# Batch 0's norm, expert choice, ranks and first four scatters moved earlier at the end of attentions 3 and 4

## What is computed

```python
q = layernorm(x) @ w_q ; k, v = ctx @ w_kv            # 16 heads of 64, ctx of 154 tokens
x = x + softmax(q k^T * scale) v @ w_out               # attention
xn = layernorm(x)
logits = xn.reshape(-1, 128) @ wg                      # 2048 tokens, 8 experts
top_vals, top_idx = top_k(logits, 2)
weights = softmax(top_vals)
x = x + sum over the 2 choices of weights * expert(top_idx)(xn)
```

## Time and profile before

| | us |
|---|---|
| median of 3 runs | 1202.76 (1201.64 to 1203.77) |
| the profiled execution, its own time | 1204.15 |
| span of its trace | 1202.4 |
| busy: PE, DVE, ACT, POOL | 1024.1, 729.6, 641.0, 573.5 |
| mean granted TensorE clock | 0.912 of full |

### The profile page before, as it was taken

How to read it: one execution, slowest core, us unless ns; L and a number is a source line. 1 busy time by engine, 2 the same in 40 slices (tenths; PEclk the granted TensorE clock), 3 DMA queues, 4 the chain that set the end, 5 groups by cost and what they waited for, 6 DMA issues and landing times.

```text
span 1202.4 us, 21878 instructions
## 1 busy us (share of the span) xinstructions
PE 1024.1 (85%) x6653; PEld 790.4 (66%) x6653; DVE 729.6 (61%) x2451; ACT 641.0 (53%) x2115; POOL 573.5 (48%) x923
## 2 busy tenths in 40 slices
PE   4986999858899988968999997697599999976993
PEld 3864888735556567855677765686467777655993
DVE  5575344576766684277767777523876767754443
ACT  2215333336777834428887875233487888831231
POOL 5232566542000023548565666657475555664452
PEclk9986999967999987989999999698799999975997
DMA  2003456696910113220000000275200000014666
GB/s 64 13 19 99 149 166 194 213 139 232 388 37 2 36 45 116 65 68 19 1 19 2 19 2 25 69 221 146 73 19 2 2 1 2 2 41 124 190 209 189
DMA packets 116003, 102.83 MB, mean 86 GB/s; under 512 B 18027, under 2 KB 97571, under 8 KB 115888
## 3 DMA queue, kind: packets, MB, share of 16 engines
q1 hardware_dynamic: 104992, 82.45, 23.5%
q0 software_dynamic: 8448, 17.20, 4.3%
q10 hardware_dynamic: 2448, 1.80, 0.7%
HBM read 65.04 MB, written 36.36 MB: 84 GB/s over the span
## 4 chain that ended last, share of the span: by engine, by line
PE 57%; DVE 16%; POOL 8%; issue 6%; DMA 6%; ACT 5%; SPq 1%; DVEq 0%; POOLq 0%; ACTq 0%
PE ps L2695 4%; PE ps L2877 4%; PE ps L2697 4%; PE ps L2696 4%; PE ps L2891 4%; PE ps L2775 3%; PE ps L2788 3%; PE ps L3065 3%; DMA xr<-xr_d,src_i 2%; POOL yq_d L902 2%; PE ps L2905 2%; POOL xq_d L883 2%; ACT ex L1278 2%; PE ps L3416 2%; PE ps L3221 2%
## 5 line engine op out<-in xcount | busy, mean ns | idle before, releaser
L1278 ACT ACTIVATE ex<-ps,nmx 128x154 f32<-128x154 f32 x512 | 193.9, 391 | 70.2 <-DVE nmx L2199 68.7
L1065 POOL TENSOR_TENSOR pp<-ex,rc 128x256 f32<-128x256 f32 x256 | 157.6, 615 | 145.5 <-DVE rc L2204 144.7
L2199 DVE TENSOR_REDUCE nmx<-ps 128x2 f32<-128x308 f32 x256 | 119.4, 469 | 61.7 <-PE ps L2697 61.3
L2877 PEld LDWEIGHTS ps<-ident,pp 128*128 128x128 f32 x640 | 73.8, 142 | 57.5 <-POOL pp L1066 49.3
L2695 PE MATMUL ps<-kp,q_s 128*128 128x308 f32 x256 | 96.4, 377 | 14.9 <-ACT ex L1278 7.7
L902 POOL DMA_INDIRECT yq_d<-yq,ids_q x78 | 74.7, 957 | 71.6 <-DVE yq L1961 52.9
L1278 ACT ACTIVATION_READ_ACCUMULATOR ex<-ps,nmx 128x1 f32 x512 | 105.1, 205 | 0.0
L2877 PE MATMUL ps<-ident,pp 128*128 128x128 f32 x640 | 100.0, 280 | 4.8 <-POOL pp L1066 4.8
L1402 ACT ACTIVATE pe<-ps,nmx 128x154 f32<-128x154 f32 x256 | 84.4, 395 | 29.4 <-DVE nmx L2080 28.4
L872 POOL TENSOR_TENSOR ln_r<-ln_v,mhalf 128x4 f32<-128x4 f32 x32 | 34.7, 1084 | 95.7 <-DVE ln_v L1696 77.6
L2696 PE MATMUL ps<-kp,q_s 128*128 128x308 f32 x256 | 79.8, 312 | 0.0
(11 more groups left out here) (448 smaller groups left out, 2756.0 us busy)
## 6 DMA issues: line engine op xcount, KB each, us to landing
w_r<-in_L_ffn_W SPq DMA_DIRECT2D x69, 256.0 KB, 3.4
xq_d<-blankq SPq DMA_DIRECT2D x4, 4160.0 KB, 23.9
w_q<-in_L_ffn_W SPq DMA_DIRECT2D x46, 256.0 KB
w_q<-in_L_ffn_w SPq DMA_DIRECT2D x46, 128.0 KB
xq<-xq_d SPq DMA_DIRECT2D x22, 130.0 KB, 2.5
w_s<-in_L_ffn_W SPq DMA_DIRECT2D x8, 256.0 KB
w_e<-in_L_ffn_W SPq DMA_DIRECT2D x8, 256.0 KB, 5.1
acc<-yq_d SPq DMA_DIRECT2D x8, 256.0 KB, 4.5
```

What stands on the lines that cost most here:

```text
L1065: pool.tensor_tensor(pp[st % 2][:, m % 4, 2 * j:2 * j + 2, :], w[:, :, 0:P], r.broadcast_to([P, 2, P]), ALU.mult)
L1278: ins = act.activation(ex[:, tt % NEX, j, :], ps[:, tt % 3, j * SK:(j + 1) * SK], ACT.Exp, bias=nmx8[:, tt % 8, j:j + 1], accum_out=sm8[:, ...
L2199: dve.tensor_reduce(nmx8[:, tt % 8, :], ps[:, tt % 3, 0:2 * SK].rearrange("p (h s) -> p h s", h=2), AX.X, ALU.max, negate=True).then_inc(n ...
L2877: last = pe.transpose(ps[:, bank, k * P:(k + 1) * P], pp[st % 2][:, k, c, :], ident[:, :])
```

## The change

In attentions 3 and 4:

- Batch 0's `tail_shift` takes the place of its `tail_scale`, and `scale(l, 0)` runs on ScalarE behind the last exponentials of step 13. The count that `shifted` waits for grows with it.
- `tail_statistics` of batches 0 and 1 stand ahead of the maxima of tile 4 in steps 13 and 14, where they stood ahead of those of tile 7. Their `rstd` on GpSimd move from behind tile 7 to behind tile 4 (step 13) and tile 5 (step 14).
- Batch 0's `tail_xT` moves from the end of step 14 to behind its tile 1, its `logits` from step 15 into step 14, `best` ahead of tile 7 of step 14, `indices` and `marks` behind tile 7 of step 14.
- `rank(0)`, `shares(0)`, `ranks(0)` and `second_rows(0)` move from the tail into step 15.
- The first four of batch 0's eight scatters are issued by GpSimd in step 15, one behind each of the tiles 4 to 7. Batch 2's `rstd` still stands behind the second scatter of those in `region`.
- The places in the ring of banks move accordingly.

```diff
--- before.py
+++ after.py
@@ -73,12 +73,12 @@
 
     ORDER = [(g, b) for g in range(2) for b in range(B)] + [(2, 0), (2, 1), (3, 0), (3, 1), (2, 2), (3, 2), (2, 3), (3, 3)]
     LAST = [max(st for st in range(NST) if ORDER[st][1] == b) for b in range(B)]
-    BEHIND = {(0, "A"): [("x", 1)], (0, "C"): [("x", 2)], (2, "A"): [("x", 3)], (13, "A"): [("f", 0)], (14, "A"): [("f", 1)], (14, "D"): [("t", 0)], (15, "A"): [("lg", 0)], (15, "D"): [("t", 1)]}
+    BEHIND = {(0, "A"): [("x", 1)], (0, "C"): [("x", 2)], (2, "A"): [("x", 3)], (13, "A"): [("f", 0)], (14, "A"): [("f", 1), ("t", 0)], (14, "C"): [("lg", 0)], (15, "A"): [("rk", 0)], (15, "D"): [("t", 1)]}
 
     BEHIND1 = {(14, "D"): [("u", 0)], (15, "A"): [("f", 0)], (15, "D"): [("u", 1)]}
     TAIL = [("f", 1), ("t", 0), ("pt", NST - 1, 3), ("o", NST - 2), ("pt", NST - 1, 1), ("pt", NST - 1, 2), ("u", 2), ("pt", NST - 1, 4), ("f", 2), ("t", 1), ("t", 2), ("o", NST - 1), ("u", 3), ("f", 3), ("t", 3)]
     NEXT = [("next", 0, i) for i in range(PREPS)]
-    ENDING = [None, None] + [[("pt", NST - 1, 1), ("rk", 0), ("pt", NST - 1, 4), ("pt", NST - 1, 3), ("f", 2), ("lg", 1), ("y", NST - 2), ("pt", NST - 1, 2), ("rk", 1), ("t", 2), ("y", NST - 1), ("lg", 2), ("f", 3)]
+    ENDING = [None, None] + [[("pt", NST - 1, 1), ("pt", NST - 1, 4), ("pt", NST - 1, 3), ("f", 2), ("lg", 1), ("y", NST - 2), ("pt", NST - 1, 2), ("rk", 1), ("t", 2), ("y", NST - 1), ("lg", 2), ("f", 3)]
                              + NEXT[0:1] * (l == 2) + [("rk", 2), ("t", 3), ("lg", 3)] + NEXT[1:2] * (l == 2) + [("rk", 3)] + NEXT[2:] * (l == 2) for l in (2, 3)]
 
     def ring(l):
@@ -597,7 +597,7 @@
 
         def shifted(l, b):
 
-            return ln_shift, B + (B - 1) * (l - 2) + b
+            return ln_shift, B + B * (l - 2) + b + 1
 
         def nth(s):
 
@@ -884,9 +884,9 @@
 
             def region(l):
 
-                for i in range(2 * TB):
+                for i in range(4, 2 * TB):
                     scatter_rows(l, 0, i)
-                    if i == 1:
+                    if i == 5:
                         rstd(2 * l + 1, 2)
                 for i in range(2 * TB):
                     scatter_rows(l, 1, i)
@@ -1104,10 +1104,12 @@
                             low_x(3)
                         elif (st, m) == (4, 0):
                             row_ids()
-                        elif (st, m) == (13, 7):
+                        elif (st, m) == (13, 4):
                             rstd(2 * l + 1, 0)
-                        elif (st, m) == (14, 7):
+                        elif (st, m) == (14, 5):
                             rstd(2 * l + 1, 1)
+                        elif st == 15 and m >= 4:
+                            scatter_rows(l, 0, m - 4)
                     if st % B == 1 and st < NST - B:
                         if st >= 2:
                             pool.wait_ge(*full(l, ("y", st - 2)))
@@ -1323,9 +1325,15 @@
                         turned_x(1)
                     elif st == 2:
                         turned_x(3)
+                    elif st == 14:
+                        tail_xT(l, 0)
+                    elif st == 15:
+                        shares(l, 0)
                     exps(st, 2)
                     copy_pt(st - 1, 2)
                     exps(st, 3)
+                    if st == 15:
+                        second_rows(l, 0)
                     exps(st, 4)
                     exps(st, 5)
                     copy_pt(st - 1, 4)
@@ -1337,14 +1345,14 @@
                         scale(l, 1)
                     step_prep(st, 3)
                     exps(st, 7)
+                    if st == 13:
+                        scale(l, 0)
                     high_out(st - 1, 0)
-                    if st >= 14:
-                        tail_xT(l, st - 14)
+                    if st == 15:
+                        tail_xT(l, 1)
                     copy_pt(st, 0)
                 high_out(NST - 2, 1)
-                shares(l, 0)
                 copy_pt(NST - 1, 4)
-                second_rows(l, 0)
                 copy_pt(NST - 1, 2)
                 shares(l, 1)
                 high_out(NST - 1, 0)
@@ -2304,13 +2312,11 @@
                         tail_sum(l, st - 13)
                     elif st == 15:
                         tail_shift(l, 1)
-                        best(l, 0)
+                        ranks(l, 0)
                     maxima(st, 3)
                     copy_pt(st - 1, 3)
-                    if st == 14:
-                        tail_scale(l, 0)
-                    elif st == 15:
-                        indices(l, 0)
+                    if st in (13, 14):
+                        tail_statistics(l, st - 13)
                     maxima(st, 4)
                     if st == 0:
                         summed_up(3)
@@ -2326,17 +2332,19 @@
                     step_prep(st, 2)
                     if st == 0:
                         moments_half(3, 1)
-                    elif st in (13, 14):
-                        tail_statistics(l, st - 13)
-                    elif st == 15:
-                        marks(l, 0)
+                    elif st == 13:
+                        tail_shift(l, 0)
+                    elif st == 14:
+                        best(l, 0)
                     maxima(st, 7)
                     step_prep(st, 3)
+                    if st == 14:
+                        indices(l, 0)
+                        marks(l, 0)
                 maxima(NST, 0)
                 copy_pt(NST - 1, 1)
                 low_out(NST - 2, 0)
                 low_out(NST - 2, 1)
-                ranks(l, 0)
                 copy_pt(NST - 1, 3)
                 tail_sum(l, 2)
                 best(l, 1)
@@ -2942,8 +2950,10 @@
                         turned_x(3)
                     elif st in (13, 14):
                         tail_sum(l, st - 13, *summed(l, st - 13))
+                        if st == 14:
+                            tail_xT(l, 0)
                     elif st == 15:
-                        logits(l, 0)
+                        rank(l, 0)
                     scores(st, 2)
                     transposes(st - 1, 2)
                     scores(st, 3)
@@ -2956,17 +2966,18 @@
                     step_prep(st, 2)
                     if st == 0:
                         turned_x(2)
+                    elif st == 14:
+                        logits(l, 0)
                     scores(st, 6)
                     step_prep(st, 3)
                     scores(st, 7)
                     values(st - 1, 1)
                     rest_values(st - 1)
-                    if st >= 14:
-                        tail_xT(l, st - 14)
+                    if st == 15:
+                        tail_xT(l, 1)
                     transposes(st, 0)
                 st = NST - 1
                 transposes(st, 1)
-                rank(l, 0)
                 transposes(st, 4)
                 transposes(st, 3)
                 tail_sum(l, 2, *summed(l, 2))
```

## The result

| | us |
|---|---|
| before, median of 9 runs | 1204.07 (1201.64 to 1206.98) |
| changed, median of 9 runs | 1215.37 (1208.97 to 1221.07) |
| ratio | 1.0085, interval 1.0063 to 1.0107 |
| the profiled execution after, its own time | 1221.07 |
| span of its trace | 1219.3 |

The change makes the kernel slower, by 11.3 us on the medians, about twice the 5.1 us of the forecast, and outside its range.

The account below looks back on a forecast made before the run. The TensorE, ScalarE, VectorE chain to batch 3's variance and ranks bounds the tail. Steps plus GpSimd's scatters less the margin gave +2.36 and +2.78, together +5.14 us: 1207.9 us on the median of 1202.76, range 1202.5 to 1212.5.

Parts of the forecast that it names:

- Bound of the tail: Tail of both attentions: the TensorE, ScalarE, VectorE chain to batch 3's variance and ranks ends last; four fewer queued scatters buy nothing.
- 1.64 us as all that the boundary costs: Boundary 13/14, attention 3: ScalarE's batch 0 scalings delay the copy VectorE awaits, +1.64 us, bounds 0 and 1.64.
- the sentence on the statistics ahead of tile 4: Step 13: batch 0's statistics, 1.37 us, make the step wait about 1.06 us, covered at the boundary by the scalings' 1.64.
- Step 14: Attention 3: VectorE's scalings leave, -1.11; batch 1's statistics, `best` and `indices` 0; marks +1.26, idle time filled -1.17, TensorE's banks and logits +0.3.
- The 0.3 for the new order of the banks: TensorE in step 14: transposes 3 wait for `tail_sum(1)` and `logits(0)` stands ahead of tile 6, +0.3 us.
- GpSimd's stretch: Step 15, tiles 4 to 7: three scatters of 1.30 us between tiles, 7.3 us in all, +1.47 and +2.12 us.
- The margin: Before the tail's transposes 4: GpSimd's last tile is ready 1.04 us early in both attentions; this is subtracted from the lateness.
- The clock: Rival, chance 0.08: TensorE's new idle stretch lowers its clock at the tail's start, +8 us on top, about 1216.
- Room: Rival, chance 0.17: steps late only some 0.7 us per attention, scatters cost a bare 0.97 us; +1.0, 1203.8 us.
- Faster: Rival, chance 0.12: steps hide everything; step 14 loses its 0.80 us stall, the tail 1.14 us; -3.9, 1198.9 us.

Follow-up runs that it names:

- the filled kernel: Changed kernel plus six unread TensorE products ahead of transposes 4 of step 15 and six ahead of batch 2's turned rows; 1.0064, 0.9995 and 0.9986 of the kernel before.

## Why the forecast was right in direction and short in size

**Bound of the tail: right.** A shorter queue waits for the chain; the forecast's signs for it came (waits before batch 1's first scatter and batch 3's `rstd`, the latter at 757.37), and with the four scatters behind the step again attention 4's last one stood 1.80 us sooner than in the filled kernel of the same chip, by just what the step was shorter.

**The step that failed first: "if `tail_shift(0)` has to wait for its `rstd`, that is a few tenths under ScalarE's cover", and with it 1.64 us as all that the boundary costs.** The shift stands ahead of tile 7's maximum, and ScalarE's scalings stand behind tile 7's exponentials; they cannot cover what delays the exponentials themselves. The scalings were rightly sized (1.54 us measured). What was put at nothing is the 1.02 and 1.44 us in front of them, 0.73 and 1.17 of it by the shift's place, so that the boundary cost 2.54 and 2.72 us. The same error stands in the sentence on the statistics ahead of tile 4, whose lateness "the 1.64 us cover": most of it is made good by tile 7, because the statistics no longer stand in front of that tile, but the 0.29 and 0.27 us that are left add to the scalings too. This step is 0.90 of the 1.26 us that attention 3's steps were short.

**Step 14: mis-sized.** The forecast had -1.11 for the scalings (measured -1.02 and -0.93), and for the choice +1.26 - 1.17 + 0.3 in steps 14/15 and +1.01 in step 15, together 1.40; measured were 1.98 and 2.02 in step 14 and 0.3 back in step 15. The idle time of VectorE was filled, as the forecast had it, but by 2.32 us of indices and marks; it counted 1.26 for the marks and nothing for the indices. The 0.3 for the new order of the banks shows as a wait of 0.35 us. Sum up to tile 4 of step 15: 3.19 and 3.50 us, for 1.93 and 1.7. For attention 4 the forecast took less than attention 3's sum, on the word that VectorE has a little room at the boundary; it had 0.26 us, but the shift's place cost 0.44 us more there than in attention 3.

**GpSimd's stretch: right, a little too large.** 1.26 and 1.87 us measured, 1.47 and 2.12 forecast. The rule of the Trainium skill, "SBUF — State Buffer", section "SBUF: two separate sides", that certain VectorE instructions keep GpSimd from writing the descriptors of its DMAs, would by the forecast's reading have made the scatters between the tiles longer. They took 1.09, 1.02 and 1.01 us, the one in the plain queue 1.02: the trace shows nothing of it here.

**The margin: right.** Tile 7 is 4.45 and 5.37 us late in the first profiles; less 1.04 this makes 3.4 and 4.3 us, and the filled kernel's last scatters were 3.71 and 4.40 us late. With the sizes put right the forecast's own mechanism gives 7.7 to 8.1 us, and the filled kernel measured 1.0064, 7.7 us (4.9 to 10.6 by its interval).

**The clock: wrong chance.** The other 3.6 us of the median (11.3 less 7.7) fit the clock, but the number itself is not shown: it compares ratios of different chips, 1.0085 and 1.0064, whose intervals overlap. For it speak the last scatters, 5.9 and 2.1 us later in two profiles of the changed kernel than in the filled one's, 4.0 in the mean. On the one chip that had both kernels the fill took 0.76% away, of which the tails show about half. The forecast gave this rival 0.08, because the new idle stretch is shorter than that of the earlier trace rows, and 8 us for two full falls; what came is a fall in some tails, of 4.7 to 5.0 us each, in three of twelve at its worst place (three of six in attention 4, none in attention 3) and later in others; the wider spread (1208.97 to 1221.07) fits that. It should have been a term of the sum with its own weight, not a case beside it. What the Trainium skill states in "TensorE: Matmul & The Clock Gate", Part 1, that the low clock is the default and activity releases the high one, agrees with the fills, behind which the clock stayed at 1.00 in the 12 us behind tile 7 in eight of eight tails.

*Room* and *Faster* fell with the first rows of the boundary. The change does what it says: the four scatters in step 15 found only 0.17 us of idle time before them, so batch 0's slots were ready.

## What to carry to other kernels

Work that is moved into an idle place must be looked up by what stands behind it on its own engine and who waits for that: a wait ahead of one engine's work and a piece behind another's are in series, not one under the other. Before a queue is shortened, ask what it would wait for next: here `rstd` and the slots of the later batches met it within tenths of a us, so the saved 5 us per attention could not arrive. And a new idle stretch of TensorE is to be priced twice, by its length and, as a chance times a price, by the clock behind it; six useless products in the gap are a cheap test of the second, best run with the same fill in the kernel before on the same chip.

## What was not expected of the hardware

The clock's fall is not a fixed property of a program. With the same order of work and stages that agree within 0.06 us up to tile 7 of step 15, the granted clock of the next 6 us was 0.64, 1.00 and 0.69 in three profiles of the changed kernel. What decides it is open.

Two of the five chips take 1246 and 1254 us for the kernel that takes 1204 on the others. Their compute stages up to step 15 are the same to 0.06 us; VectorE and ScalarE have waits of 1.3 to 9.1 us around the tails there, and more of the kind elsewhere, released by something that the trace calls remote; none of the traces of the other chips has such a wait. VectorE's timeline of the filled kernel on such a chip, at batch 3's ranks, whose rank bank had long been full:

```profile
784.22 0.19 DVE L1871 TENSOR_TENSOR pick<-ps,oh 128x32 f32<-128x32 f32 x1 [7.13 <-remote]
```

Such a wait may hide a part of what comes before it, and the changed kernel is at 1.0062 there, for 1.0085 and 1.0090; but the fill looks larger there, not smaller, so this is not shown. What the wait is was not settled.
